# A routed feed-forward kernel on one core: x tile ahead of side columns, the first product's passes reordered, ScalarE's and VectorE's first pair reordered, a quarter of the mixing moved ahead of the first product

## The chip, the cores and the metric

The kernel runs on one core of one Trainium2 chip. The metric is the device time of one execution in microseconds. Before the change the median of three runs is 959.52 us (959.34 to 960.11).

## What is computed

The reference, cut to what matters (`x` is 128 x 64 x 1024 in float32; there are 8 conditioning kernels, 8 experts of rank 16, and 2 experts are chosen for each row):

```python
h = gelu(cond @ W0 + b0); h = gelu(h @ W1 + b1)
att = softmax(h @ W2 + b2)
agg_w = einsum('bk,koi->boi', att, weight)
y = einsum('boi,bih->boh', agg_w, x) + (att @ bias_k)[:, :, None]

base = einsum('bsd,od->bso', y, base_W)
probs = softmax(einsum('bsd,ed->bse', y, router_W))
w_dense = weights of the top 2 of probs, divided by their sum
mid = einsum('bsd,edr->bser', y, lora_A) * w_dense[..., None]
out = x + base + 2 * einsum('bser,erd->bsd', mid, lora_B)
```

## The kernel before

The rows (128 x 64) are taken in 64 tiles of 128 rows, two tiles to a "pair", 32 pairs. For each pair TensorE first mixes: `y = agg_w x`, with a 128 x 128 matrix `mix_w` for each tile. This is done in four quarters of four 128-column chunks (`mix_chunk(n, q, j)`, L483 to L497; quarter q reads `x_sb[q % 2]` and writes `y_ps[q % 2]`), and VectorE's `add_bias(n, q)` (L1122) moves a quarter from PSUM to `ya`, adding `bias_sb`. Then comes the large product of y with `base_W`. Each float32 operand is split into a high part (rounded, written by ScalarE, `*_hi`) and a low part (the rest, a subtraction on VectorE, `*_lo`), and each product is three passes: high by high, high by low, low by high. The blocks of the operand y are named A11, A12, A21, A22 and those of the weights B11, B21, B12, B22. From pair 2 on a seven-product scheme with sums of blocks (S1 to S4, T1 to T4) is used; pairs 0 and 1 use plain products (`plain_pair`, L623). The side columns (`side`, the columns of `lora_A` and of the router) are multiplied along: a product with them is a "head" of 376 columns (`plain_head`, L543) and a "tail" of 272 columns (`plain_tail`, L549), which holds the rest of the block and the side columns, and so needs the side columns' parts `side_hi_set` and `side_lo_set`. VectorE then chooses the experts from the logits (`route_logits`, `route_choice`, `route_weigh`, with `exponents` on ScalarE), makes `mid`, and `lora_B` (`lb_hi`, `lb_lo`) is multiplied with `mid`'s high and low parts.

There is no scheduler. The program of each engine is written out in its order, and engines wait for each other on semaphores; an engine that waits lets nothing behind it pass. What the change touches is the start, pair 0:

- SP (L266 to L278) issues the first loads on one queue: parameters, a block of weights (`a_raw`, B11), `x_sb[0]`, the side columns, `x_sb[1]`, three more blocks, `lora_B`, and a block for T1. `next_x(1)` (L280) loads pair 1's x tiles when quarters 2 and 3 of pair 0 have been mixed; `next_bias(1)` (L286) loads `bias_sb` for pair 1, after `bias_out`.
- GpSimd (POOL) makes the high and low parts of B11 (L366, L369), one half each at a time. Later it issues transfers that add a negated block to another in place (`add_to`, L372).
- TensorE mixes quarters 0 and 1, issues two warming matmuls (`keep_warm(2)`, L501), and enters `first_product` (L564), then a small bias product (L638), quarters 2 and 3, and the product of A21.
- ScalarE's `first_pair` (L964) and VectorE's `first_pair` (L1273) are lists of splits, negations and copies. The parts of a block of weights are written over the raw block in places, so a low part of B22 (`take_lo(B22, n)`) must wait until ScalarE has negated it (`neg_b22_set`). `keep_biases` (L920) copies the bias rows and issues their transfer to memory, at whose end `bias_out` rises.

Of the kernel before, what the change touches and what calls it, by code (L numbers as in the profile page):

```python
# [5 lines left out]
def adaln_ffn_kernel(nc, x, params, mix_t, bias_k, base_t, side, lora_b, out):  # L6
# [30 lines left out]
    HALF = 4  # L37
    WP = 2
# [19 lines left out]
    with ctx:  # L58
# [207 lines left out]
        def _(sp):  # L266
# [2 lines left out]
            sp.dma_start(bk_sb[:, :], bias_k).then_inc(bk_in, 16)  # L269
            sp.dma_start(a_raw, base_t[0, :, :]).then_inc(a_in, 16)  # L270
            sp.dma_start(x_sb[0][:, :], x_t[0, :, :]).then_inc(x_in[0], 16)
            sp.dma_start(w_raw[W_SIDE], side).then_inc(side_in, 16)
            sp.dma_start(x_sb[1][:, :], x_t[1, :, :]).then_inc(x_in[1], 16)
            sp.dma_start(b_raw, base_t[2, :, :]).then_inc(b_in, 16)
            sp.dma_start(c_raw, base_t[1, :, :]).then_inc(c_in, 16)
            sp.dma_start(d_raw, base_t[3, :, :]).then_inc(d_in, 16)
# [164 lines left out]
        def _(pe):  # L441
            def keep_warm(times):

                for _ in range(times):
                    nc.tensor.matmul(pb[:, 0:BANK], hot[:, 0:P], hot[:, :], start=True, stop=True)
# [52 lines left out]
            for q in range(2):  # L498
                for j in range(HALF):
                    mix_chunk(0, q, j)  # L500
            keep_warm(2)  # L501
            SPLITS = ((op_hi, w_hi), (op_hi, w_lo), (op_lo, w_hi))

            def wait_operand(o, p):
# [38 lines left out]
            def plain_head(y, w, start, stop, blk, to, j):  # L543

                at = blk * BLOCK + j * BANK
                nc.tensor.matmul(to[:, LEAD:BANK], y, w[:, at:at + HEAD], start=start, stop=stop,  # L546
                                 skip_group_check=True)
# [16 lines left out]
            def first_product():  # L564

                hi, lo = op_hi[A11], op_lo[A11]
                passes = [list(plain_splits(hi, lo, j, True)) for j in range(HALF)]
                pe.wait_ge(a11_first_set, 1)
                pe.wait_ge(op_hi_set[A11], 1)
                pe.wait_ge(w_hi_set[B11], WP)  # L570
                pe.wait_ge(side_hi_set, 1)
                for j in range(HALF):
                    plain_head(*passes[j][0], B11, pa, j)
                    plain_tail(*passes[j][0], B11, pa, j, 0)
                pe.wait_ge(op_lo_set[A11], 1)
                for j in range(HALF):
                    plain_head(*passes[j][2], B11, pa, j)
                    plain_tail(*passes[j][2], B11, pa, j, 0)
                for j in range(HALF):
                    if j % (HALF // WP) == 0:  # L580
                        pe.wait_ge(w_lo_set[B11], j // (HALF // WP) + 1)
                    plain_head(*passes[j][1], B11, pa, j)
                pe.wait_ge(side_lo_set, 1)
                for j in range(HALF):
                    plain_tail(*passes[j][1], B11, pa, j, 0)
# [37 lines left out]
            def plain_pair(p):  # L623
# [10 lines left out]
                if first(p):  # L634
                    first_product()
                    pe.wait_ge(bk_in, 16)
                    pe.wait_ge(bias_set, 2)
                    nc.tensor.matmul(bias_ps, att_t[:, :], bk_sb[:, :], start=True, stop=True).then_inc(bias_mm, 1)  # L638
                    for q in range(2, 4):
                        for j in range(HALF):  # L640
                            mix_chunk(0, q, j)
                else:
                    wait_operand(A11, p)
                    pe.wait_ge(plain_out, 1)
                    for j in range(HALF):
                        plain_with_side(*a11, B11, pa, j, 0, True)
# [208 lines left out]
        def _(act):  # L855
# [50 lines left out]
                               bias_bc[:, m * P:(m + 1) * P].rearrange("p (b s c) -> p b s c", s=2, b=PAR)  # L906
                               ).then_inc(bias_set, 1)
            place_mix(0, 1)
            act.wait_ge(side_in, 16)
            nc.scalar.activation(w_hi[W_SIDE], w_raw[W_SIDE], ACT.Copy).then_inc(side_hi_set, 1)  # L910

            def first_a11_high(m, done):

# [50 lines left out]
            def first_pair():  # L964
                first_a11_high(0, a11_first_set)
                first_a11_high(1, op_hi_set[A11])
                split_a21(0)
                act.wait_ge(att_rows_mm, 1)
                nc.scalar.copy(att_rows[:, :], pb[:, BANK:]).then_inc(att_rows_set, 1)
                act.wait_ge(b_in, 16)  # L970
                for n in range(WP):
                    take_hi(B21, n)
                keep_biases()
                split_high(A12, 0, y_ready, 4)
                split_high(A22, 0, y_ready, 4)
                act.wait_ge(a_in, 16)
                negate(T2, 0, neg_b11_set)
                act.wait_ge(c_in, 16)
                for n in range(WP):
                    nc.scalar.activation(w_hi[w_piece(T4, n)], w_raw[w_piece(T3, n)], ACT.Copy  # L980
                                         ).then_inc(b12_hi_set, 1)
                act.wait_ge(d_in, 16)
                for n in range(WP):
                    take_hi(B22, n)
                for m in range(2):
                    place_mix(1, m)
                negate(B22, 1, neg_b22_set)
                exponents(0)
                act.wait_ge(lb_in, 16)
                nc.scalar.activation(lb_hi[:, :], lb_raw[:, :], ACT.Copy).then_inc(lb_hi_set, 1)  # L990
                exponents(1)
# [68 lines left out]
        def _(dve):  # L1060
# [212 lines left out]
            def first_pair():  # L1273
# [20 lines left out]
                route_logits(0, pa[:, SLOG])  # L1294
                route_choice(0)
                route_weigh(0, pa[:, SMID])
                dve.wait_ge(neg_b22_set, WP)
                for n in range(WP):
                    take_lo(B22, n)
                add_bias(1, 0)  # L1300
                dve.wait_ge(lb_hi_set, 1)
                nc.vector.tensor_tensor(lb_lo[:, :], lb_raw[:, :], lb_hi[:, :].bitcast(f32),
                                        ALU.subtract).then_inc(lb_lo_set, 1)
# [157 lines left out]
```

## Time and profile before

| | us |
|---|---|
| median of the three runs | 959.52 |
| the profiled execution | 959.47 |
| its span, first to last instruction | 957.6 |
| TensorE (PE) busy | 949.1 (99%) |
| VectorE (DVE) busy | 741.8 (77%) |
| GpSimd (POOL) busy | 295.8 (31%) |
| ScalarE (ACT) busy | 237.8 (25%) |

The profile was taken in one execution. Times in the trace are microseconds from the span's start. The granted TensorE clock is 1.00 in all of the first 40 us. PEld is TensorE's loading of weights, which overlaps the matmuls. In a timeline a row is one instruction or several alike in a sequence (x4): its start, its length, engine, line, operation, what is written and read, the shapes, and in brackets for how long the engine sat idle before it and what ended that. Matmuls are pipelined: a recorded length runs past the start of the next, so that the time of a matmul in a sequence is read from start to start. In the chain of work the lengths add up.

### The profile page before, as it was taken

What the parts mean: (1) busy time and instruction counts of PE and PEld (TensorE: products, weight loads), DVE (VectorE), ACT (ScalarE), POOL (GpSimd) and SP (SyncE); (2) the same over time, 40 slices, a digit from 0 to 9 for tenths busy, and PEclk for the clock granted to TensorE, in tenths of its full rate; (3) what the DMA queues carried; (4) which work ended last, traced back from release to release, by engine and by line L of the source; (5) the groups of instructions that cost most, each with busy time, mean ns of one, the idle gap of its engine ahead of it and who ended that gap; (6) DMA issues with size and microseconds to landing.
All of it is one profiled execution on the core that took longest, in us unless ns stands there. A gap on an engine that the chain in (4) does not pass through costs nothing.

```text
span 957.6 us, 17843 instructions
## 1 busy us (share of the span) xinstructions
PE 949.1 (99%) x5777; PEld 876.6 (92%) x5777; DVE 741.8 (77%) x1641; ACT 237.8 (25%) x546; POOL 295.8 (31%) x230
## 2 busy tenths in 40 slices
PE   7999999999999999999999999999999999999998
PEld 6999999999999999999999999999999999999997
DVE  5778877877777877778777778777778777787775
ACT  5444222222212222222222122222222222222220
POOL 3012333123332133332233331333321333312331
PEclk9999999999999999999999999999999999999999
DMA  9766234423234332333332343333343323433311
GB/s 349 202 191 176 80 108 140 133 96 106 99 115 137 110 115 93 104 126 134 110 110 78 115 137 122 102 104 105 115 136 110 114 82 104 137 133 99 110 44 66
DMA packets 47125, 116.04 MB, mean 121 GB/s; under 512 B 20480, under 2 KB 20864, under 8 KB 45952
## 3 DMA queue, kind: packets, MB, share of 16 engines
q1 hardware_dynamic: 46112, 111.41, 35.0%
q0 software_dynamic: 576, 4.19, 2.3%
q8 instruction: 12, 0.20, 0.1%
q10 hardware_dynamic: 416, 0.16, 0.1%
q14 instruction: 9, 0.07, 0.0%
HBM read 77.97 MB, written 33.59 MB: 116 GB/s over the span
## 4 chain that ended last, share of the span: by engine, by line
PE 98%; DMA 1%; SPq 0%; issue 0%; ACT 0%; DVE 0%
PE pc L518 17%; PE pa L529 13%; PE pb L529 13%; PE y_ps L493 12%; PE pb L532 9%; PE pa L532 9%; PE pd L518 9%; PE pd L609 5%; PE pc L609 4%; PE pc L591 1%; PE pd L591 1%; DMA x_sb<-in_x 1%; PE pa L546 1%; PE pb L546 1%; PE pd L599 1%; PE pa L554 1%
## 5 line engine op out<-in xcount | busy, mean ns | idle before, releaser
L493 PE MATMUL y_ps<-mix_w,x_sb 128*128 128x128 f32 x1024 | 193.5, 273 | 1.0 <-DMA x_sb<-in_x 0.9
L409 POOL TENSOR_TENSOR out_sb<-out_sb,u 128x512 f32<-128x512 f32 x90 | 127.8, 1450 | 202.0 <-DVE u L1239 202.0
L493 PEld LDWEIGHTS y_ps<-mix_w,x_sb 128*128 128x128 f32 x1024 | 166.9, 188 | 13.3 <-DMA x_sb<-in_x 1.1
L379 POOL TENSOR_TENSOR ya<-ya 128x512 f32<-128x512 f32 x30 | 40.0, 1334 | 380.2 <-DVE ya L1142 380.2
L1142 DVE TENSOR_TENSOR ya<-y_ps,bias_sb 128x512 f32<-128x512 f32 x128 | 87.8, 686 | 38.3 <-PE y_ps L493 34.7
L518 PE MATMUL pc<-w_hi,s_hi 128*128 128x512 f32 x236 | 97.5, 413 | 0.0
L529 PE MATMUL pa<-w_hi,a_hi 128*128 128x376 f32 x240 | 94.6, 394 | 0.7 <-ACT p L956 0.7
L518 PE MATMUL pc<-w_hi,s_lo 128*128 128x512 f32 x236 | 92.8, 393 | 0.0
L518 PE MATMUL pc<-w_lo,s_hi 128*128 128x512 f32 x236 | 92.2, 391 | 0.0
L941 ACT ACTIVATE exps<-logits,neg_max 128x8 f32<-128x8 f32 x64 | 19.3, 301 | 260.6 <-DVE neg_max L1161 260.6
L948 ACT ACTIVATE mid_hi<-pd 128x128 fp32r<-128x128 f32 x61 | 16.9, 278 | 269.9 <-PE pd L599 269.9
L529 PE MATMUL pa<-w_hi,a_lo 128*128 128x376 f32 x240 | 80.2, 334 | 0.0
L529 PE MATMUL pa<-w_lo,a_hi 128*128 128x376 f32 x240 | 80.2, 334 | 0.0
L1153 DVE TENSOR_TENSOR a_lo<-ya,a_hi 128x512 fp32r<-128x512 f32 x96 | 67.9, 708 | 10.0 <-ACT a_hi L937 9.4
L532 PE MATMUL pa<-w_hi,a_hi 128*128 128x272 f32 x240 | 69.0, 288 | 0.0
L532 PE MATMUL pa<-w_lo,a_hi 128*128 128x272 f32 x240 | 69.0, 287 | 0.0
L532 PE MATMUL pa<-w_hi,a_lo 128*128 128x272 f32 x240 | 69.0, 287 | 0.0
L937 ACT ACTIVATE a_hi<-ya 128x512 fp32r<-128x512 f32 x95 | 59.5, 627 | 20.9 <-DVE ya L1142 20.9
L1204 DVE TENSOR_TENSOR out_sb<-pc,out_sb 128x512 f32<-128x512 f32 x92 | 62.5, 681 | 0.7 <-PE pc L609 0.7
L937 ACT ACTIVATE s_hi<-ya 128x512 fp32r<-128x512 f32 x60 | 37.7, 628 | 77.8 <-PE pb L532 77.1
L518 PE MATMUL pd<-w_hi,s_hi 128*128 128x512 f32 x120 | 56.8, 474 | 0.0
L1221 DVE TENSOR_TENSOR side_b<-pb,p 128x136 f32<-128x136 f32 x30 | 9.0, 300 | 60.7 <-PE pb L532 60.7
(236 smaller groups left out, 2561.1 us busy)
## 6 DMA issues: line engine op xcount, KB each, us to landing
x_sb<-in_x SPq DMA_DIRECT2D x64, 512.0 KB, 3.3
out_sb<-in_x SPq DMA_DIRECT2D x64, 512.0 KB, 4.4
out<-out_sb SPq DMA_DIRECT2D x62, 512.0 KB, 2.8
w_raw<-in_base_t SPq DMA_DIRECT2D x5, 1024.0 KB, 12.7
w_raw<-neg POOLq DMA_DIRECT2D x4, 1024.0 KB, 12.7
bias_sb<-bias_rows SPq DMA_DIRECT2D x62, 64.0 KB, 4.9
out<-out_sb SPq DMA_DIRECT2D x3, 256.0 KB, 2.0
w_raw<-in_side SPq DMA_DIRECT2D x1, 544.0 KB, 8.9
```

Source lines behind the costliest of these rows:

```text
L379: nc.gpsimd.tensor_tensor(y_block(0, 1), y_block(0, 1), y_block(0, 0), ALU.subtract).then_inc(s3_set, 1)
L409: nc.gpsimd.tensor_tensor(o, o, u2[:, :], ALU.add).then_inc(done, 1)
L493: mm = nc.tensor.matmul(y_ps[q % 2][:, j * P:(j + 1) * P], x_sb[m][:, c * P:(c + 1) * P], mix_w[m][:, :], start=True, stop=True)
L518: mm = nc.tensor.matmul(to[:, 0:BANK], y[o][:, j * P:(j + 1) * P], w[:, at:at + BANK], start=(begin and j == 0 and n == 0), stop=(j == HAL ...
L529: nc.tensor.matmul(to[:, LEAD:BANK], y[o][:, j * P:(j + 1) * P], w[:, at:at + HEAD], start=start, stop=stop, skip_group_check=True)
L532: mm = nc.tensor.matmul(to[:, BANK:BANK + 2 * SD].rearrange("p (a n) -> p a n", a=2), y[o][:, j * P:(j + 1) * P], tail, start=start, stop= ...
L609: mm = nc.tensor.matmul(to[:, :], m[:, :], w[:, cols], start=(begin and n == 0), stop=(n == 2), skip_group_check=True)
L937: nc.scalar.activation(op_hi[o][:, :], OPERAND[o], ACT.Copy).then_inc(op_hi_set[o], 1)
L941: nc.scalar.activation(exps[:, :], logits[:, :], ACT.Exp, bias=neg_max[:, :]).then_inc(exps_ready, 1)
L1142: nc.vector.tensor_tensor(to[:, :, :, m, :], y_ps[q % 2][:, :].rearrange("p (j s r) -> p j s r", j=HALF, s=2), bias_sb[m][:, :].rearrange( ...
L1153: nc.vector.tensor_tensor(op_lo[o][:, :], OPERAND[o], op_hi[o][:, :].bitcast(f32), ALU.subtract).then_inc(op_lo_set[o], 1)
L1204: nc.vector.tensor_tensor(o, src, o, ALU.add).then_inc(done, 1)
```

## The change

Five things are moved and nothing is added or removed. On SP `x_sb[1]` is loaded ahead of the side columns. On TensorE quarter 2 of pair 0's mixing stands ahead of the first product, and the first product runs its heads by themselves (high by high; half of high by low; low by high; the other half of high by low), and then the twelve tails. On ScalarE the high part of the side columns stands behind the two high parts of A11, the negation of B11 ahead of the bias rows and of A12, `place_mix(1, m)` ahead of B22, and `exponents(0)` ahead of the negation of B22. On VectorE `add_bias(1, 0)` stands ahead of the low parts of B22, whose wait is for each half by itself.

```diff
@@ SP
+            sp.dma_start(x_sb[1][:, :], x_t[1, :, :]).then_inc(x_in[1], 16)
             sp.dma_start(w_raw[W_SIDE], side).then_inc(side_in, 16)
-            sp.dma_start(x_sb[1][:, :], x_t[1, :, :]).then_inc(x_in[1], 16)
@@ TensorE
             keep_warm(2)
+            for j in range(HALF):
+                mix_chunk(0, 2, j)
@@ TensorE, first_product
                 pe.wait_ge(a11_first_set, 1)
                 pe.wait_ge(op_hi_set[A11], 1)
                 pe.wait_ge(w_hi_set[B11], WP)
+                def low_weights(n):
+                    pe.wait_ge(w_lo_set[B11], n + 1)
+                    for j in range(n * HALF // WP, (n + 1) * HALF // WP):
+                        plain_head(*passes[j][1], B11, pa, j)
+
+                for j in range(HALF):
+                    plain_head(*passes[j][0], B11, pa, j)
+                low_weights(0)
+                pe.wait_ge(op_lo_set[A11], 1)
+                for j in range(HALF):
+                    plain_head(*passes[j][2], B11, pa, j)
+                low_weights(1)
                 pe.wait_ge(side_hi_set, 1)
-                for j in range(HALF):
-                    plain_head(*passes[j][0], B11, pa, j)
-                    plain_tail(*passes[j][0], B11, pa, j, 0)
-                pe.wait_ge(op_lo_set[A11], 1)
-                for j in range(HALF):
-                    plain_head(*passes[j][2], B11, pa, j)
-                    plain_tail(*passes[j][2], B11, pa, j, 0)
-                for j in range(HALF):
-                    if j % (HALF // WP) == 0:
-                        pe.wait_ge(w_lo_set[B11], j // (HALF // WP) + 1)
-                    plain_head(*passes[j][1], B11, pa, j)
+                for n in (0, 2):
+                    for j in range(HALF):
+                        plain_tail(*passes[j][n], B11, pa, j, 0)
                 pe.wait_ge(side_lo_set, 1)
                 for j in range(HALF):
                     plain_tail(*passes[j][1], B11, pa, j, 0)
@@ TensorE, plain_pair
-                    for q in range(2, 4):
-                        for j in range(HALF):
-                            mix_chunk(0, q, j)
+                    for j in range(HALF):
+                        mix_chunk(0, 3, j)
@@ ScalarE
             place_mix(0, 1)
-            act.wait_ge(side_in, 16)
-            nc.scalar.activation(w_hi[W_SIDE], w_raw[W_SIDE], ACT.Copy).then_inc(side_hi_set, 1)
...
                 first_a11_high(1, op_hi_set[A11])
+                act.wait_ge(side_in, 16)
+                nc.scalar.activation(w_hi[W_SIDE], w_raw[W_SIDE], ACT.Copy).then_inc(side_hi_set, 1)
                 split_a21(0)
...
                     take_hi(B21, n)
+                act.wait_ge(a_in, 16)
+                negate(T2, 0, neg_b11_set)
                 keep_biases()
                 split_high(A12, 0, y_ready, 4)
                 split_high(A22, 0, y_ready, 4)
-                act.wait_ge(a_in, 16)
-                negate(T2, 0, neg_b11_set)
...
+                for m in range(2):
+                    place_mix(1, m)
                 act.wait_ge(d_in, 16)
                 for n in range(WP):
                     take_hi(B22, n)
-                for m in range(2):
-                    place_mix(1, m)
+                exponents(0)
                 negate(B22, 1, neg_b22_set)
-                exponents(0)
@@ VectorE
                 route_weigh(0, pa[:, SMID])
-                dve.wait_ge(neg_b22_set, WP)
+                add_bias(1, 0)
                 for n in range(WP):
+                    dve.wait_ge(neg_b22_set, n + 1)
                     take_lo(B22, n)
-                add_bias(1, 0)
```

How the instructions stand at the two places with most to do. TensorE, from the end of the mixing's quarter 1 (`x_sb_54` is `x_sb[1]`, `x_sb_53` is `x_sb[0]`; `pa` is the first product's bank) to the first product's wait for the low part of A11; before:

```order
17 L493 MATMUL y_ps<-mix_w_79,x_sb_54 128x128 [waits mix_set1,x_in1]
18 L493 MATMUL y_ps<-mix_w_79,x_sb_54 128x128 x3
19 L445 MATMUL pb<-hot 128x512 x2
20 L546 MATMUL pa<-w_hi,a_hi 128x376 [waits w_hi_set0,side_hi_set,op_hi_set0,a11_first_set]
21 L554 MATMUL pa<-w_hi,a_hi 128x272
22 L546 MATMUL pa<-w_hi,a_hi 128x376
23 L554 MATMUL pa<-w_hi,a_hi 128x272
24 L546 MATMUL pa<-w_hi,a_hi 128x376
25 L554 MATMUL pa<-w_hi,a_hi 128x272
26 L546 MATMUL pa<-w_hi,a_hi 128x376
27 L554 MATMUL pa<-w_hi,a_hi 128x272
28 L546 MATMUL pa<-w_hi,a_lo 128x376 [waits op_lo_set0]
```

and now:

```order
19 L445 MATMUL pb<-hot 128x512 x2
20 L493 MATMUL y_ps<-mix_w_78,x_sb_53 128x128 [waits y_ready]
21 L493 MATMUL y_ps<-mix_w_78,x_sb_53 128x128 x3
22 L548 MATMUL pa<-w_hi,a_hi 128x376 [waits w_hi_set0,op_hi_set0,a11_first_set]
23 L548 MATMUL pa<-w_hi,a_hi 128x376 x3
24 L548 MATMUL pa<-w_lo,a_hi 128x376 [waits w_lo_set0]
25 L548 MATMUL pa<-w_lo,a_hi 128x376
26 L548 MATMUL pa<-w_hi,a_lo 128x376 [waits op_lo_set0]
27 L548 MATMUL pa<-w_hi,a_lo 128x376 x3
28 L548 MATMUL pa<-w_lo,a_hi 128x376 [waits w_lo_set0]
29 L548 MATMUL pa<-w_lo,a_hi 128x376
30 L556 MATMUL pa<-w_hi,a_hi 128x272 [waits side_hi_set]
```

Quarter 2's four chunks stand ahead of the product, the wait for the side columns has gone from the first matmul to the first tail, and six heads instead of four heads and four tails stand ahead of the wait for the low part of A11 (`op_lo_set0`).

ScalarE, from the copy of the side columns or the high parts of A11 to the high parts of B12, before:

```order
17 L910 ACTIVATE w_hi<-w_raw 128x1088 [waits side_in]
18 L916 ACTIVATE a_hi<-ya 128x4x64 [waits y_ready] x2
19 L962 ACTIVATE a_hi<-ya 128x512 [waits y_ready]
20 L969 COPY att_rows<-pb 128x512 [waits att_rows_mm]
21 L861 ACTIVATE w_hi<-w_raw 128x1024 [waits b_in]
22 L861 ACTIVATE w_hi<-w_raw 128x1024
23 L923 COPY bias_rows_sb<-pd 128x64 [waits bias_mm]
24 L925 DMA bias_rows<-bias_rows_sb 128x2x32 [waits bias_ready]
25 L937 ACTIVATE a_hi<-ya 128x512 [waits y_ready] x2
26 L867 ACTIVATE neg_106<-w_raw 128x1024 [waits a_in]
27 L867 ACTIVATE neg_106<-w_raw 128x1024
28 L980 ACTIVATE w_hi<-w_raw 128x1024 [waits c_in]
```

and now:

```order
17 L919 ACTIVATE a_hi<-ya 128x4x64 [waits y_ready] x2
18 L971 ACTIVATE w_hi<-w_raw 128x1088 [waits side_in]
19 L965 ACTIVATE a_hi<-ya 128x512 [waits y_ready]
20 L974 COPY att_rows<-pb 128x512 [waits att_rows_mm]
21 L866 ACTIVATE w_hi<-w_raw 128x1024 [waits b_in]
22 L866 ACTIVATE w_hi<-w_raw 128x1024
23 L872 ACTIVATE neg_106<-w_raw 128x1024 [waits a_in]
24 L872 ACTIVATE neg_106<-w_raw 128x1024
25 L926 COPY bias_rows_sb<-pd 128x64 [waits bias_mm]
26 L928 DMA bias_rows<-bias_rows_sb 128x2x32 [waits bias_ready]
27 L940 ACTIVATE a_hi<-ya 128x512 [waits y_ready] x2
28 L985 ACTIVATE w_hi<-w_raw 128x1024 [waits c_in]
```

The copy of the side columns has gone behind the high parts of A11, and the two negations (`neg_106`) ahead of the bias rows' copy and transfer.

## Rows read from the trace of the kernel before

**Rows 1.** The chain of work that ended last: shares of the span by engine.
```profile
PE 98%; DMA 1%; SPq 0%; issue 0%; ACT 0%; DVE 0%
```
**Rows 2.** Waits of TensorE over the span: us in total, times, longest.
```profile
PE pa L529 <- ACT p L956: 0.7, 1, 0.7
```
**Rows 3.** Timeline of TensorE, 13 to 22 us.
```profile
13.27 1.16 PE L493 MATMUL y_ps<-mix_w,x_sb 128*128 128x128 f32 x8 [0.90 <-DMA x_sb<-in_x]
14.19 0.71 PE L445 MATMUL pb<-hot 128*128 128x512 f32 x2
15.78 0.41 PE L546 MATMUL pa<-w_hi,a_hi 128*128 128x376 f32 x1 [0.88 <-issue]
...
19.53 0.43 PE L638 MATMUL pd<-bk_sb,att_t 8*128 8x64 f32 x2
19.89 2.05 PE L493 MATMUL y_ps<-mix_w,x_sb 128*128 128x128 f32 x16
21.70 0.42 PE L546 MATMUL pb<-w_hi,a_hi 128*128 128x376 f32 x1
```
**Rows 4.** The chain in order of time: start, us, what.
```profile
18.41 0.69 PE pa L546 x4
...
29.95 0.09 issue
30.05 0.46 PE y_ps L493 x2
...
31.39 0.22 PE y_ps L493 x2
```
**Rows 5.** Timeline of ScalarE.
```profile
11.99 0.51 ACT L880 COPY mix_w<-summed 64x64 f32<-64x64 f32 x2
12.52 1.11 ACT L910 ACTIVATE w_hi<-w_raw 128x1088 fp32r<-128x1088 f32 x1
...
20.24 0.44 ACTq L925 DMA_DIRECT2D bias_rows<-bias_rows_sb  x1
...
29.45 1.03 ACT L880 COPY mix_w<-summed 64x64 f32<-64x64 f32 x4
```
**Rows 6.** Timeline of SP, whose rows are the issues of transfers.
```profile
3.01 0.44 SPq L272 DMA_DIRECT2D w_raw<-in_side  x1
...
24.66 0.90 SPq L290 DMA_DIRECT2D bias_sb<-bias_rows  x2
```
**Rows 7.** From issue to landing, us: side columns; pair 1's `bias_sb` (its tile's view).
```profile
w_raw<-in_side SPq DMA_DIRECT2D x1, 544.0 KB, 8.9
...
DMA to landing us min/median/max: 5.8/7.9/10.0
```
**Rows 8.** Timeline of VectorE.
```profile
14.54 0.69 DVE L1142 TENSOR_TENSOR ya<-y_ps,bias_sb 128x512 f32<-128x512 f32 x1 [1.37 <-PE y_ps L493]
15.78 0.98 DVE L1153 TENSOR_TENSOR a_lo<-ya,a_hi 128x512 fp32r<-128x512 f32 x1 [0.55 <-ACT a_hi L916]
...
33.89 2.35 DVE L1064 TENSOR_TENSOR w_lo<-w_raw,w_hi 128x1024 fp32r<-128x1024 f32 x2
...
40.40 0.28 DVE L1199 TENSOR_TENSOR mid_lo<-pd,mid_hi 128x128 fp32r<-128x128 f32 x1
...
80.83 4.36 DVE L1064 TENSOR_TENSOR w_lo<-w_raw,w_hi 128x1024 fp32r<-128x1024 f32 x2
```
**Rows 9.** Timeline of GpSimd.
```profile
11.53 4.69 POOL L369 TENSOR_TENSOR w_lo<-w_raw,w_hi 128x1024 fp32r<-128x1024 f32 x2
...
80.25 1.63 POOL L397 TENSOR_TENSOR s<-s,ya 128x512 f32<-128x512 f32 x1
81.84 2.27 POOL L400 TENSOR_TENSOR ya<-ya,s 128x512 f32<-128x512 f32 x1
```
**Rows 10.** Timeline of TensorE, 33 to 42 us.
```profile
33.45 0.38 PE L493 MATMUL y_ps<-mix_w,x_sb 128*128 128x128 f32 x2
...
41.03 0.42 PE L617 MATMUL pa<-lb_hi,mid_hi 128*128 128x376 f32 x1
```

More of the change, by code:

```diff
@@ L570, in first_product @@
                 pe.wait_ge(w_hi_set[B11], WP)
-                pe.wait_ge(side_hi_set, 1)
+                def low_weights(n):
+                    pe.wait_ge(w_lo_set[B11], n + 1)
+                    for j in range(n * HALF // WP, (n + 1) * HALF // WP):
+                        plain_head(*passes[j][1], B11, pa, j)
                 for j in range(HALF):
                     plain_head(*passes[j][0], B11, pa, j)
-                    plain_tail(*passes[j][0], B11, pa, j, 0)
+                low_weights(0)
                 pe.wait_ge(op_lo_set[A11], 1)
@@ L577, in first_product @@
                     plain_head(*passes[j][2], B11, pa, j)
-                    plain_tail(*passes[j][2], B11, pa, j, 0)
-                for j in range(HALF):
-                    if j % (HALF // WP) == 0:
-                        pe.wait_ge(w_lo_set[B11], j // (HALF // WP) + 1)
-                    plain_head(*passes[j][1], B11, pa, j)
+                low_weights(1)
+                pe.wait_ge(side_hi_set, 1)
+                for n in (0, 2):
+                    for j in range(HALF):
+                        plain_tail(*passes[j][n], B11, pa, j, 0)
                 pe.wait_ge(side_lo_set, 1)
```

## The prediction

> **What bounds the kernel now.** Read the chain of work first: 98% of it is TensorE [rows 1], so a part of the change counts only where it removes or makes an idle stretch of TensorE. The view of waits comes next: the last one of TensorE in the whole span that it lists is 0.7 us for ScalarE's copy of `pa` [rows 2]; that copy follows TensorE's own product, in the third pair, and moves with it. All others lie before the first product. What the change can win is therefore at the start, which the timelines show.
>
> TensorE mixes quarter 1 of pair 0 at 13.27, after 0.90 us of waiting for the transfer of `x_sb`; two warming matmuls follow at 14.19; the first product starts at 15.78, after 0.88 us of waiting [rows 3]. At 19.53 stands the bias product, at 19.89 quarters 2 and 3 of the mixing, 1.81 us together, and at 21.70 the second product [rows 3]. Nothing waits between 15.78 and 21.70. One small wait more: the first mixing matmuls of pair 1 start at 30.05 when ScalarE's two copies into `mix_w` (half of 1.03 us from 29.45, so 29.95) are done. In the chain they take 0.46 us instead of 0.22, after a gap of 0.09: 0.33 us of waiting in all [rows 4, 5].
>
> **x ahead of the side columns.** The side columns, issued at 3.01, landed 8.9 us later, at 11.9 [rows 6, 7]; the second x tile, next on the queue, just before the 13.27 of the matmul that waited for it [rows 3]. One tile is 512 KB and the side columns are 544 KB, so changing places lets x land at about 11.9 and the side columns at 13.2. Then another thing is last: the second `mix_w` is written by ScalarE at 11.99 + 0.51 = 12.50 [rows 5]. With the 0.1 us from the end of such a copy to its matmul, 29.96 to 30.05 [rows 4, 5], quarter 1 starts at 12.6, 0.67 us sooner. VectorE's bias add, ScalarE's second high part of A11 and the head that waits for it follow each other directly, so the add goes from 14.54 to 13.87 and the first product from 15.78 to 15.11 [rows 3, 8]. ScalarE's copy of the side columns (1.11 us [rows 5]) now stands behind that high part, 15.0 to 16.1, on data that landed at 13.2.
>
> **The third quarter of mixing ahead of the first product.** Its condition, one finished bias add, is met at 13.2. It starts behind the two warming matmuls (recorded 0.71 us from 14.19, so from 13.52 then) at 14.0 to 14.2 and takes half of 1.81 us, to 15.1 at the latest, inside what was a wait. This takes 0.90 us from after the first product. It also sets free `x_sb` for the load of pair 1 some 6 us sooner, but that load stands behind the weights on the same queue of SP, and so should land as before.
>
> **The first product's order.** The work is the same, 12 matmuls of 376 columns ("heads") and 12 of 272 ("tails"), 15.78 to 19.53 = 3.75 us without a wait; a head takes 0.17 us (four in 0.69 [rows 4]), and for the first after a wait I allow 0.08 more. Now four heads with high parts and two with the low weights (GpSimd's first half, ready after half of 4.69 us from 11.53, at 13.9 [rows 9]) run from 15.11 to 16.2 (6 x 0.17 + 0.08 = 1.10). Then the low part of A11 is wanted. Here is the choice on which the number hangs. VectorE's subtraction for it ran from 15.78 to 16.76, 0.98 us, where the add of the same size at 14.54 took 0.69; GpSimd's two subtractions ran to 11.53 + 4.69 = 16.22 [rows 8, 9]. 16.76 is 0.54 us behind that end, within one undisturbed instruction. The same is seen at 80.83: two VectorE subtractions take 4.36 us, where two like them took 2.35 at 33.89, beside two of GpSimd [rows 8, 9]. Let each engine wait for the other's whole instruction: VectorE waits to 81.88, works 1.07 us; GpSimd waits for that and ends at 84.11; VectorE's second ends 1.08 us later, at 85.19, the recorded end. So I take it that VectorE does not get through before GpSimd ends: however early it is asked, the low part is ready at 16.76. The Trainium skill (SBUF — State Buffer, section "SBUF: two separate sides") has such a rule: a VectorE instruction with two SBUF inputs and a GpSimd one that reads SBUF share a pair of ports under an exclusive lock, and the later of the two is blocked until the other ends. By that rule, the trace agreeing at both places, the head start that the change gives this subtraction is spent on waiting, and the sum stays 1.25 us; were the engines only slowed, it would be 1.9 us, rival 1.
>
> TensorE then waits from 16.2 to 16.86, and has 3.75 - 1.10 = 2.65 us left, to 19.51: only 0.02 us sooner than now. The side columns' low parts (VectorE, directly behind, of 1088 columns, so little over half of the 2.35 us of 33.89, to 18.0) are wanted at 19.0; no wait. Bias product 0.36 us, quarter 3 0.90 us: the second product starts at 20.78 against 21.70, **0.92 us sooner**.
>
> **ScalarE's first pair reordered.** ScalarE starts on A21's high part later now, by the side copy, and, its instructions laid end to end from 16.1, ends the high parts of B21 at about 19.1 and the negation of B11 at 21.0. VectorE follows as now, since its low part of A11 is not sooner. By my estimate from the rows of like size A12 is ready at about 23.5 and wanted some 3.6 us (twelve pairs of head and tail) after 20.8: covered. `place_mix` for pair 1 now runs before B22, done for its first tile at about 26.0 and wanted at 28.8: **the 0.33 us at 30.05 goes**. The negation of B22 goes behind `exponents(0)`, ending near 31.8. All this is cover at no price: if B22's low part were late it would show as a wait of `pc<-w_lo` at 36.
>
> **VectorE's bias add first.** `add_bias(1, 0)` now stands before B22's low parts. It waits for TensorE's mixing quarter, whose last matmuls end at 33.83 now [rows 10] and at 32.6 then, and for `bias_sb`. Queued behind it are B22's low parts, `lb_lo`, the second routing and `mid_lo`; these and the add took from 33.89 to 40.68, 6.8 us, without a wait [rows 8]: `mid_lo` at 39.5. TensorE wants it at 41.03 - 1.25 = 39.8 [rows 10]: covered, by 0.2 to 0.3 us.
>
> **Sum.** 0.92 + 0.33 = 1.25 us. The profiled execution took 959.47 us (span 957.60 and 1.87 around it), 0.05 below the median of the three runs, 959.52. It gives 958.22 and 958.27: I say 958.3. About 0.2%, 1.9 us, is what a measurement can tell from no change, so this is "the same".
>
> **Rivals.** (1) VectorE is not held up: it works slower beside GpSimd but ends 0.98 us after it starts. The low part is then ready at 15.11 + 0.98 = 16.09, TensorE never waits, and the gain is 1.25 + 0.65 = 1.9 us: 957.6. For it: the durations overlap in the record. Against it: both places give ends that fit exclusion to 0.05 us. Chance 0.15, half of it past the bound.
>
> (2) The other side: `bias_sb` is late and holds VectorE's queue. ScalarE issued the copy of the bias rows to memory at 20.24 [rows 5], and SP the load that waits for it at 24.66 [rows 6]; now the copy stands behind the negation, at about 21.25, and the load at 25.7. Its first half landed 5.8 us after its issue and the second 10.0 [rows 7]. With 5.8 it lands at 31.5, with 10.0 at 35.7; VectorE wants it at 32.6. Past 32.8 each microsecond is one of TensorE's, past 34.1 the gain is gone; at 35.7 TensorE's wait is 2.9 us and the time 959.52 - 1.25 + 2.9 = 961.2, and past 36.0 it is slower by over 0.2%. For it: GpSimd's accumulating transfer of T1 is no longer held by the negation of B11 and starts up to 2 us sooner, closer to this load. Against it: the load stands behind pair 1's two x tiles, as now, and those come no later. Chance 0.10, half of it slower than before, a quarter past the bound.
>
> (3) Only the mixing quarter is won and something small comes back (B21's or A12's parts, `mid_lo` by its 0.2 us of cover): 0.25 to 1.2 us less gain, 958.6 to 959.5. Chance 0.20. That the order does nothing at all is excluded, as the quarter does move into a wait of 0.9 us.
>
> The forecast itself has 0.55. The transfers' landings can shift by a few tenths.
>
> **How the numbers follow.** The range reaches down to rival 1 with 0.1 us for noise, 957.5, and up through rival 3 with 0.2 us for the spread of runs, 959.7; outside are most of rival 2 and little else. Faster by over 0.2% (under 957.6): half of rival 1 and little of the rest, 0.10. Slower by over 0.2% (over 961.4): 0.04. Else 0.86.
>
> **What would show it.** In the timeline after: quarter 1 at 12.6; quarter 2 of the mixing at 14.0; first head at 15.1; VectorE's first `a_lo` lasting about 1.6 us and ending at 16.76; a wait of TensorE of 0.65 us before the first `w_hi,a_lo`; second product at 20.8; no wait at the first mixing matmuls of pair 1 (28.8); every later TensorE row 1.25 us sooner. An `a_lo` that ends near 16.1 would prove rival 1; an add of pair 1 that begins after 32.8, ended by a transfer, rival 2. A time under 957.5 or over 959.7 would prove the sum wrong.

## The result and the profile after

| | before | after |
|---|---|---|
| median, us | 959.52 (22 runs, 959.31 to 960.12) | 961.44 (22 runs, 958.33 to 963.72) |
| the profiled execution, us | 959.47 | 961.68 |
| its span, us | 957.6 | 959.8 |

The ratio is 1.0019, with a 95% interval of 1.0013 to 1.0025: the change makes the kernel slower, by 1.9 us or 0.2%, which is about the least that can be told from no change. It also spreads the runs over 5.4 us where they lay within 0.8. The granted clock is 1.00 in both profiled executions.

The waits of TensorE over the span of the changed kernel (us in total, times, longest), but for 2.7 us and 0.2 us at the very start:

```profile
PE pc L597 <- DVE w_lo L1069: 1.7, 1, 1.7
PE pa L623 <- DVE mid_lo L1204: 1.1, 1, 1.1
PE pa L531 <- ACT p L959: 0.7, 1, 0.7
PE pa L548 <- DVE a_lo L1158: 0.4, 1, 0.4
PE y_ps L493 <- ACT mix_w L885: 0.3, 1, 0.3
```

The first two are what no part of the forecast had: VectorE is late with the low parts of B22 and with `mid_lo`. The last two are the wait for the low part of A11, which was forecast, and a short one that follows x's earlier landing. The chain of work, by engine:

```profile
PE 96%; DMA 2%; DVE 1%; ACT 1%; issue 0%; POOL 0%; DVEq 0%; POOLq 0%
```

It was 98% TensorE [rows 1]. The 2% of transfers are two. The same chain in order of time (start, us, what):

```profile
19.00 1.89 ACT neg L872 x2
20.89 0.11 ACT bias_rows_sb L926
21.02 6.84 DMA bias_rows<-bias_rows_sb
27.87 8.34 DMA bias_sb<-bias_rows
...
36.29 0.06 DVE ya L1147
...
36.90 2.35 DVE w_lo L1069 x2
39.25 1.13 DVE lb_lo L1307
...
42.82 0.29 DVE mid_lo L1204
43.11 0.14 issue
43.24 0.41 PE pa L623
```

This is one path from end to end: ScalarE's negation, the copy of the bias rows to memory (6.8 us), the load of `bias_sb` that waits for it (8.3 us), VectorE's first bias add of pair 1, and all that is queued behind that add. TensorE's timeline, with the rows that answer to [rows 3, 4, 10]:

```profile
12.71 1.13 PE L493 MATMUL y_ps<-mix_w,x_sb 128*128 128x128 f32 x8 [0.27 <-ACT mix_w L885]
...
14.14 1.05 PE L493 MATMUL y_ps<-mix_w,x_sb 128*128 128x128 f32 x8
15.19 0.93 PE L548 MATMUL pa<-w_hi,a_hi 128*128 128x376 f32 x4
15.96 0.51 PE L548 MATMUL pa<-w_lo,a_hi 128*128 128x376 f32 x2
16.84 0.97 PE L548 MATMUL pa<-w_hi,a_lo 128*128 128x376 f32 x4 [0.37 <-DVE a_lo L1158]
...
20.87 0.42 PE L548 MATMUL pb<-w_hi,a_hi 128*128 128x376 f32 x1
...
28.97 0.38 PE L493 MATMUL y_ps<-mix_w,x_sb 128*128 128x128 f32 x2
...
38.16 0.50 PE L597 MATMUL pc<-w_hi,a_hi 128*128 128x512 f32 x1 [1.70 <-DVE w_lo L1069]
...
43.24 0.41 PE L623 MATMUL pa<-lb_hi,mid_hi 128*128 128x376 f32 x1 [1.14 <-DVE mid_lo L1204]
```

Up to 28.97 all goes as forecast to within 0.2 us: the mixing of pair 1 starts 1.08 us sooner than in [rows 4]. Then the product with `lora_B` starts at 43.24 against 41.03 [rows 10], 2.21 us later, and 2.2 us is what the span grew by. VectorE, for [rows 8]:

```profile
15.20 1.59 DVE L1158 TENSOR_TENSOR a_lo<-ya,a_hi 128x512 fp32r<-128x512 f32 x1 [0.55 <-ACT a_hi L919]
...
36.29 0.69 DVE L1147 TENSOR_TENSOR ya<-y_ps,bias_sb 128x512 f32<-128x512 f32 x1 [4.68 <-DMA bias_sb<-bias_rows]
36.90 2.35 DVE L1069 TENSOR_TENSOR w_lo<-w_raw,w_hi 128x1024 fp32r<-128x1024 f32 x2
```

Finally the three issues that matter, on ScalarE's queue, SP's and GpSimd's (for [rows 5, 6]; GpSimd's stood at 26.37 before):

```profile
21.02 0.47 ACTq L928 DMA_DIRECT2D bias_rows<-bias_rows_sb  x1
27.87 1.71 SPq L290 DMA_DIRECT2D bias_sb<-bias_rows  x2
25.39 1.01 POOL L374 DMA_DIRECT2D w_raw<-neg  x1 [9.16 <-DMA w_raw<-in_base_t]
```

The load of `bias_sb` is issued 3.2 us later than before, and GpSimd's accumulating transfer of T1 (1 MB) 1.0 us sooner. The load used to be issued 1.7 us ahead of T1's transfer; now it comes 2.5 us behind it. How the DMA queues fared between 27 and 31 us (queue and kind: packets, MB, share of the 16 engines' time; q0 is GpSimd's, q1 is SP's), before:

```profile
q1 hardware_dynamic: 409, 0.37, 37.3%
```

and after:

```profile
q0 software_dynamic: 109, 0.89, 113.0%
q10 hardware_dynamic: 10, 0.00, 0.2%
q1 hardware_dynamic: 1, 0.00, 0.0%
```

### The profile page after: what moved, and what is told of

The parts are those of the page before. It is cut to its first block, busy times and chain, and to the rows that moved or that the text cites. A ratio compares the mean times of both kernels' runs of the same rounds, so it can differ in the third digit from the quotient of the medians.

```text
span 959.8 us, 17843 instructions
## 1 busy us (share of the span) xinstructions
PE 949.8 (99%) x5777; PEld 876.9 (91%) x5777; DVE 742.3 (77%) x1641; ACT 238.0 (25%) x546; POOL 295.7 (31%) x230
## 4 chain that ended last, share of the span: by engine, by line
PE 96%; DMA 2%; DVE 1%; ACT 1%; issue 0%; POOL 0%; DVEq 0%; POOLq 0%
PE pc L520 17%; PE pa L531 13%; PE pb L531 13%; PE y_ps L493 11%; PE pb L534 9%; PE pa L534 9%; PE pd L520 9%; PE pd L615 5%; PE pc L615 4%; PE pd L597 1%; DMA bias_sb<-bias_rows 1%; DMA bias_rows<-bias_rows_sb 1%; PE pd L605 1%; PE pc L597 1%; PE pb L445 0%; PE pb L548 0%
```

## The experiments

The first theory (A): the load of `bias_sb` loses to T1's transfer, and VectorE's add, now at the head of its queue, hands the delay on. Its rival (B): the bias rows leave later, behind the negation, and that alone makes the load late. A second rival (C): pair 1's early x load, which the moved mixing quarter lets SP issue at 15.2 in place of 21.1, crowds the queue. In the recorded expectations A1 stands for A, and D (once B') for C; "Theory C" in the first of them is another one, that ScalarE's order is at fault. No experiment leaves out or changes any part of the computation.

### One part of the change undone, or one transfer held

**VectorE's bias add back behind B22's low parts.**

```diff
-                add_bias(1, 0)
                 for n in range(WP):
                     dve.wait_ge(neg_b22_set, n + 1)
                     take_lo(B22, n)
+                add_bias(1, 0)
```

> The changed kernel with one line put back on VectorE: add_bias(1, 0) behind B22's low parts. Theory A (the transfer of pair 1's bias_sb lands at about 36.2 instead of 30.5, and VectorE, waiting for it at the head of its queue, holds back B22's low parts, lb_lo and mid_lo): B22's low parts run from about 31.6 to 34, TensorE's wait of 1.7 us before pc with w_lo goes; the add still starts near 36.3, so lb_lo, the second routing and mid_lo still follow it (4.5 us, to 40.9) and TensorE, which now wants mid_lo at 39.8, waits about 1.1 us more: 959.5, between 959 and 960. Theory C (the bias transfer is innocent, something in ScalarE's order makes B22's parts late): the time stays near 961.4.

Measured: 958.71 us (958.27 to 960.15), ratio 0.9994 (0.9985 to 1.0003). 2.7 us of the changed kernel's time are back, more than was expected of A (959 to 960), and the spread has shrunk. In the profiled execution, 958.27, the fastest of its runs, `bias_sb` landed at 33.3, against 36.2 in the changed kernel, and the add ran at 33.79 without a wait. So in most runs the loss needs the add at the head of the queue. Why some still go up to 960.15 was not seen; that a load can be late enough for an add in its old place is shown below, by the quarter alone.

**T1's transfer held until `bias_sb` has landed** (the changed kernel, one wait more on GpSimd).

```diff
                 pool.wait_ge(neg_b11_set, WP)
+                pool.wait_ge(bias_in[0], 16)
                 add_to(T1, 0, t1_made)
```

> The changed kernel, but GpSimd starts the accumulating transfer of T1 only when bias_sb of pair 1 has landed. Theory A1 (that transfer, moving from 26.6 to 32, takes the DMA engines while bias_sb waits): bias_sb, issued at 27.9, lands 3.4 to 5.8 us later, at 31.3 to 33.7, VectorE's wait of 4.7 us shrinks to under 2, and the time is 958.2 to 959.4. Theory B (bias_sb is late because its copy to memory is issued 0.8 us later and takes 6.8 instead of 4.4 us): only a part of the lateness hangs on T1, the landing stays near 36 and the time near 961.4.

Measured: 958.47 (958.28 to 960.4), ratio 0.9992 (0.9983 to 1.0001). In the profiled execution the load was issued at 27.60, hardly sooner than the 27.87 of the changed kernel, but landed in 5.9 us in place of 8.3. This speaks for A: the issue was as late, and the time was back.

**The bias rows back ahead of the negation**, the direct test of B.

```diff
+                keep_biases()
                 act.wait_ge(a_in, 16)
                 negate(T2, 0, neg_b11_set)
-                keep_biases()
```

> The changed kernel, but keep_biases is back ahead of the negation of B11 on ScalarE. The bias rows' copy to memory is issued at about 20.0 instead of 21.0. Theory B: it lands by 24.6, bias_sb is issued by 24.7 and lands by 30.5 to 31.5 as before the change; the whole loss goes, 958.2 to 958.6. Theory A1 (T1's transfer is the cause): it still begins near 26.6 and meets bias_sb, which stands behind pair 1's x tiles to 27.6; the landing is at 32 to 36 and the time 959 to 961.4.

Measured: 961.31 (960.18 to 963.53), ratio 1.002 (1.0011 to 1.003). Nothing is won: B alone falls. SP's, GpSimd's and VectorE's timelines of this kernel:

```profile
25.11 1.73 SPq L290 DMA_DIRECT2D bias_sb<-bias_rows  x2
...
23.41 1.01 POOL L374 DMA_DIRECT2D w_raw<-neg  x1 [7.17 <-ACT neg L872]
...
34.77 0.69 DVE L1147 TENSOR_TENSOR ya<-y_ps,bias_sb 128x512 f32<-128x512 f32 x1 [2.57 <-DMA bias_sb<-bias_rows]
```

The load is issued at 25.11, 2.8 us sooner than in the changed kernel, but T1's transfer is still ahead of it, at 23.41, and the load takes 9.6 us.

**Pair 1's first x load held until all of pair 0 is mixed**, the test of C.

```diff
-                    sp.wait_ge(mixed, 4 * n + m - 1)
+                    sp.wait_ge(mixed, 4 if first_load else 4 * n + m - 1)
```

> The changed kernel, but the load of x_sb[0] for pair 1 is held until all four quarters of pair 0 are mixed (about 20.9), as late as before the change. Theory D (that load, issued at 15.2 instead of 21.1, keeps SP's queue full when the bias rows go to memory, so that their copy takes 6.8 us instead of 4.4): the copy takes 4.4 to 5, bias_sb is issued at about 25.7 and the time falls to 958.3 to 960. Theories A1 and B: nothing changes by more than 0.5 us, near 961.4.

Measured: 959.97 (958.37 to 962.9), ratio 1.001 (1.0001 to 1.002): between the two, and spread over 4.5 us. In the profiled execution (961.3) T1's transfer was issued at 24.90 and the load at 28.92, after a copy of the bias rows that took 7.9 us. So the copy was no shorter for it in that execution. Holding the x load wins 1.5 us in the median, but most runs stay slower than before: it is not what decides here.

**Both cures together** (the add behind, T1's transfer held).

> The changed kernel with both cures: add_bias(1, 0) behind B22's low parts on VectorE, and GpSimd's transfer of T1 held until bias_sb of pair 1 has landed. Theory A (VectorE's wait for bias_sb, made long by T1's transfer, is the whole loss): no run is far above the fastest, the median is 958.3 (958.2 to 958.5), against 958.7 and 958.5 for the cures alone. If another cause remains, the median stays above 958.6 with runs of 959 to 960 among them.

Measured: **958.33 (958.19 to 958.54)**, ratio 0.9988 (0.9979 to 0.9997). That is the time that was forecast for the change, and the spread is gone with the loss. TensorE's product with `lora_B` starts at 39.87 there, against 41.03 before (1.16 us sooner) and 43.24 after: the changed kernel lost 3.37 us between 36 and 43 us.

### One part alone, in the kernel before

**The negation of B11 ahead of the bias rows.**

> The kernel before with one part of the change: the negation of B11 ahead of keep_biases on ScalarE. Theory A1 (the negation ahead lets T1's transfer start when T1 has landed, at 23 to 25.4 instead of 26.4, and the bias rows go out 2 us later): bias_sb lands at 33 to 36 or later instead of 30.5. In the kernel before VectorE asks for it only at 36.2, so that most of it is hidden: 959.5 to 960.0, with single runs up to 961. Theory B' (the lateness comes from the early x load or the order of SP's loads): bias_sb lands at 30.5 to 32.

Measured: 959.18 (959.04 to 960.16), ratio 0.9998 (0.999 to 1.0007). T1's transfer was issued at 24.36, ahead of the load at 25.64, and the load took 10.0 us, to 35.6. The add, still behind B22's low parts, ran at 35.74, and TensorE has no wait between 29 and 46 us: the late load is there and costs nothing. The time is even below the 959.5 to 960.0 expected, since with the negation gone from there ScalarE writes `mix_w` for pair 1 at 27.45 in place of 29.45, and TensorE's wait at that mixing is gone.

**VectorE's bias add ahead of B22's low parts.**

> The kernel before with one part of the change: add_bias(1, 0) ahead of B22's low parts on VectorE. Theory A: the place of the add is harmless as long as bias_sb lands in time, and here it lands at 30.5: the add waits for the mixing's quarter to 33.9, mid_lo is ready at 40.7 to 40.8, TensorE wants it at 41.0: 959.5 (959.3 to 959.8). Rival: the add at the head of the queue costs by itself, 0.2 us or more of waiting before the product with lora_B: 959.8 and over.

Measured: 959.44 (959.26 to 960.12 but for one far-off run), ratio 1.000 (0.9991 to 1.0009). The load was issued at 24.40, ahead of T1's transfer at 26.25, landed at 30.2, and the add ran at 33.77. The add's new place is there and costs nothing.

**Quarter 2 of the mixing ahead of the first product.**

> The kernel before with one part of the change: quarter 2 of pair 0's mixing ahead of the first product. By the prediction's sum it takes 0.90 us from behind the first product and fits into the wait ahead of it (14.7 to 15.6): 958.6 (958.4 to 958.9). If a part of it pushes the first product, the gain is 0.6 or less: 958.9 and over.

Measured: 961.03 (958.86 to 962.37 but for one far-off run); the ratio, 1.0008 (0.9999 to 1.0017), doesn't tell it from no change. This expectation was a miss: neither the negation nor the add has been moved here, and yet most runs are slower. Four of twelve lie at 958.86 to 958.94, as expected, the others from 960.3 up. The profiled execution is one of those, 962.37; SP's and VectorE's rows:

```profile
26.92 1.38 SPq L290 DMA_DIRECT2D bias_sb<-bias_rows  x2
...
38.73 0.69 DVE L1143 TENSOR_TENSOR ya<-y_ps,bias_sb 128x512 f32<-128x512 f32 x1 [3.12 <-issue]
```

The copy of the bias rows took 6.8 us in place of 4.4, so the load was issued at 26.92, behind T1's transfer (25.75), and landed after 11.7 us, at 38.6: too late even for an add in its old place. The same kernel was then run with each of the two transfers held.

**The quarter ahead, T1's transfer held.**

> The kernel before with quarter 2 of the mixing ahead of the first product (as b5, which came out at 961.0 with runs from 958.9 to 962.4), and GpSimd's transfer of T1 held until bias_sb of pair 1 has landed. Theory A1 (there too T1's transfer starves the load of bias_sb, which is issued after 26.9): bias_sb lands by 34, VectorE's add starts when its queue reaches it, no run stands far above the fastest, median 958.8 (958.7 to 959.1), the 0.6 to 0.9 us of the quarter. If T1's transfer is not the cause there: still 960 to 962.

Measured: 958.94 (958.86 to 959.37), ratio 0.9996 (0.9987 to 1.0005). The load was issued at 26.53 and took 5.9 us.

**The quarter ahead, pair 1's x load held.**

> The kernel before with quarter 2 of the mixing ahead of the first product (as b5), and the load of x_sb[0] for pair 1 held until quarter 3 is mixed, with T1's transfer as it was. Theory D (the early x load makes the bias rows' copy to memory land 6.8 us after its issue instead of 4.4, so that bias_sb is issued behind T1's transfer instead of ahead of it): the copy lands near 24.6, bias_sb is issued ahead of T1's transfer and the time is 958.8 (958.7 to 959.2). If the x load is innocent: 960 to 962 as b5.

Measured: 958.88 (958.78 to 958.97), ratio 0.9994 (0.9985 to 1.0003). The copy of the bias rows took 3.8 us, the load was issued at 23.95, ahead of T1's transfer, and took 5.6. So here C is what tips the order, and either cure is enough.

This pair shows the race most plainly, since T1's transfer was issued at the same time in both (25.75 and 25.76). The DMA queues from 27 to 31 us, the quarter alone:

```profile
q0 software_dynamic: 96, 0.79, 99.2%
```

and with the x load held:

```profile
q1 hardware_dynamic: 340, 0.36, 28.0%
```

Whichever was issued first has this stretch for itself, even where, as in the second, the engines are 28% busy. From 31 us on, in the second kernel, both move.

### The order put right without holding T1's transfer

The changed kernel with the bias rows ahead of the negation and the x load held, the add left ahead.

> The changed kernel with both things put back that delay the bias rows' copy: keep_biases ahead of the negation, and the x load held; T1's transfer is free to start when T1 has landed (23 to 25.4). Theory of a race (what counts is which of the two, the load of bias_sb or T1's transfer, is in the queues first, and the negation behind keep_biases lets T1's transfer go only after 22.8): the median falls below a3's 961.3 and a4's 960.0, to 958.4 to 959.5, with some runs above 960 left. Theory A1 in its strict form (T1's transfer alone decides): 960 to 961.5.

Measured: 959.16 (958.35 to 963.05), ratio 1.0002 (0.9992 to 1.0012). It doesn't settle: five of eleven runs lie at 958.35 to 958.87, the rest from 959.16 up. In the profiled one (958.35) SP was first by 0.13 us:

```profile
24.83 0.90 SPq L290 DMA_DIRECT2D bias_sb<-bias_rows  x2
...
24.96 1.01 POOL L374 DMA_DIRECT2D w_raw<-neg  x1 [8.71 <-DMA w_raw<-in_base_t]
...
32.72 0.69 DVE L1147 TENSOR_TENSOR ya<-y_ps,bias_sb 128x512 f32<-128x512 f32 x1 [0.51 <-PE y_ps L493]
```

The load landed in 4.6 us, and the add waited for TensorE alone. With a lead of 0.13 us the order can turn from run to run; that the slower runs are those in which it turned was not seen, since only one run is profiled.

### What all profiles say of the race

Each row is one profiled execution (the last experiment, below, went as "both cures"): when the two transfers were issued, and from issue to landing, in us. `bias_sb` is loaded in two halves; the first is meant, for which the add waits.

| kernel | `bias_sb` issued | T1's issued | `bias_sb` took | T1's took |
|---|---|---|---|---|
| before | 24.66 | 26.37 | 5.8 | 16.1 |
| add alone | 24.40 | 26.25 | 5.8 | 15.9 |
| quarter, x held | 23.95 | 25.76 | 5.6 | 16.5 |
| rows first, x held | 24.83 | 24.96 | 4.6 | 10.9 |
| T1's held | 27.60 | 34.11 | 5.9 | 9.3 |
| both cures | 26.77 | 33.10 | 5.7 | 9.4 |
| quarter, T1's held | 26.53 | 33.04 | 5.9 | 9.2 |
| add behind | 25.81 | 23.10 | 7.5 | 8.0 |
| rows first | 25.11 | 23.41 | 9.6 | 7.9 |
| negation alone | 25.64 | 24.36 | 10.0 | 9.0 |
| x held | 28.92 | 24.90 | 6.9 | 8.7 |
| **after** | 27.87 | 25.39 | 8.3 | 7.9 |
| quarter alone | 26.92 | 25.75 | 11.7 | 9.6 |

Where the load was issued first it took 4.6 to 5.9 us; where T1's transfer was, 6.9 to 11.7. In those six the load landed 2.2 to 3.4 us after T1's transfer did (after: 25.39 + 7.9 = 33.3, then 36.2). So the load's landing isn't a price of its own, as [rows 7] had seemed to give it: it depends on which of two queues was first. T1's issue moves too: with the negation ahead it waits for the load of T1's block in most profiles, and came at 23.10 to 25.39 without any edit to that load.

### VectorE beside GpSimd

The last experiment takes the reading that the sum rested on and uses it. Both cures, and GpSimd's second half of B11's low part cut in two pieces, the last of which waits until VectorE has made the low part of A11; the first product's second low weights move behind eight tails (this part of the edit isn't shown).

```diff
+            for n in (2, 3):
+                if n == 3:
+                    pool.wait_ge(op_lo_set[A11], 1)
...
+                mm = nc.gpsimd.tensor_tensor(w_lo[:, to], w_raw[:, of], w_hi[:, to].bitcast(f32), ALU.subtract)
```

> The version with both cures (958.33), and GpSimd's second half of B11's low part cut in two, its last piece held until VectorE has made the low part of A11, with the first product's second low weights behind the tails. If VectorE's subtraction is shut out while GpSimd's runs (the prediction's reading): it now starts at 15.2 and takes 0.69 us instead of 1.5 to 1.6, TensorE's wait of 0.3 to 0.6 us before the first a_lo goes, and the time is 958.0 (957.8 to 958.3). If it is only slowed by sharing, it takes about 1 us or its old 1.5; if GpSimd's late piece in turn holds VectorE's side columns, TensorE waits 0.2 to 0.5 us ahead of the last tails and nothing is won: 958.3.

Measured: **957.84 (957.75 to 957.89)**, ratio 0.9983 (0.9974 to 0.9992): 1.6 us under the kernel before, 3.6 under the changed one, and the fastest of all. Timelines of VectorE and GpSimd:

```profile
15.13 0.69 DVE L1167 TENSOR_TENSOR a_lo<-ya,a_hi 128x512 fp32r<-128x512 f32 x1 [0.55 <-ACT a_hi L928]
...
13.86 1.29 POOL L376 TENSOR_TENSOR w_lo<-w_raw,w_hi 128x512 fp32r<-128x512 f32 x1
15.90 1.29 POOL L376 TENSOR_TENSOR w_lo<-w_raw,w_hi 128x512 fp32r<-128x512 f32 x1 [0.75 <-DVE a_lo L1167]
```

With GpSimd idle the subtraction takes 0.69 us, not 1.59, TensorE no longer waits for it, and its second product starts at 20.36 against 20.87 after and 20.86 with both cures. The overlap has moved to VectorE's next subtraction, that of the side columns:

```profile
16.06 2.28 DVE L1133 TENSOR_TENSOR w_lo<-w_raw,w_hi 128x1088 fp32r<-128x1088 f32 x1 [0.24 <-ACT w_hi L980]
```

It takes 2.28 us beside GpSimd's last piece where it took 1.28 before, and nothing of TensorE's waits for it.

## Why the prediction was wrong

The forecast was 958.3, within 0.2% of before. What came is 961.44, and with it rival 2, which had a chance of 0.10: "`bias_sb` is late and holds VectorE's queue".

**The start: right.** Quarter 1 at 12.71 (12.6 forecast), quarter 2 at 14.14 (14.0), the first head at 15.19 (15.1), the second product at 20.87 (20.8), and no wait at the mixing of pair 1. Of the differences 0.07 us is a later start of the first mixing, at 11.35 against 11.28 before. The low part of A11 took 1.59 us (1.6 forecast) and ended at 16.79. The wait for it is recorded as 0.37 us; from start to start the first head behind it, at 16.84, is 0.54 us later than six heads without a wait would have put it (16.3).

**The gain: nearly right, though two parts of the change won nothing.** Both cures together give 958.33, a gain of 1.1 us where 1.25 was forecast. The quarter alone is worth 0.9 at the second product: it starts at 20.69 to 20.71 in the three kernels with the quarter alone, against 21.59 in both kernels without it (negation alone, add alone) and 21.70 before. In the three with it the first product started at 15.12, 15.58 and 15.70, as x landed sooner or later, and it made no difference: its wait for the low part of A11 took it back. With x ahead and the first product's passes reordered as well it starts at 20.86 (both cures): 0.15 us later. The sum had said of x ahead that it wins nothing ("the head start that the change gives this subtraction is spent on waiting"). The reordering loses by the rows: ahead of the same wait it puts six heads (1.1 us) where four heads and four tails (15.78 to 17.05, nearly 1.3 us) stood. The rest of the gain is ScalarE's: with the negation alone TensorE's wait at pair 1's mixing is gone already, while with the quarter alone TensorE arrives sooner at pair 1's mixing and waits 0.47 us there, so that the quarter by itself wins only 0.5 us (958.88 and 958.94).

**The step that failed** is in VectorE's part: the landing of `bias_sb`, which the sum put at no cost. It called it covered, on the ground given against rival 2, "the load stands behind pair 1's two x tiles, as now, and those come no later". The x tiles did not delay it. Issued at 25.7 and 5.8 us long, as forecast, it would have been there at 31.5; it landed at 36.2, and TensorE waited 1.7 us for B22's low parts and 1.1 us for `mid_lo`. Three things did it, each of which stood in the text by itself:

- The copy of the bias rows, issued at 21.02 (21.25 forecast), took 6.8 us, not 4.4. Only its issue had been moved in the text, and its length kept. The x load, which "should land as before", is in SP's queue from 15.2 on; with the quarter alone, holding it brings the copy from 6.8 back to 3.8 us. In the kernel with all of the change but the x load held it took 7.9, so this can't be all of it.
- T1's transfer came 1.0 us sooner. Rival 2 had this ("starts up to 2 us sooner, closer to this load") but not that the two change places. By its own figures they could: T1's transfer at 24.4 at the earliest, the load at 25.7. The load went from 1.7 us ahead to 2.5 us behind, and behind it moves only when T1's transfer is nearly done.
- The add was put at the head of VectorE's queue, with B22's low parts and `mid_lo` behind it. In the kernel before, 10.0 us for the load cost nothing (negation alone); with the add ahead, a load that took 9.6 (rows first) costs 1.9 us against both cures (960.18 and 958.31, both profiled).

The price that rival 2 gave was right. It put the point at which cover ends at a landing at 32.8; the load landed at 36.2, 3.4 us past it, and the changed kernel lost 3.37 us against the one with both cures. The other three kernels with the add ahead and a late load fit as well: landings 0.7, 1.9 and 3.0 us past 32.8 (T1's held, rows first, x held) put the product with `lora_B` at 40.52, 41.72 and 42.84, which is 0.65, 1.85 and 2.97 us behind both cures' 39.87. That its 961.2 lies near 961.44 is in part luck: the load was issued 2.2 us later than it had it and took 1.7 us less than its 10.0. What was wrong was the chance. The two landings, 5.8 and 10.0, stood in [rows 7]; the question of what made the second of them 4.2 us longer, in the kernel before, was not asked. T1's first packets moved at 31 to 32 us in that trace, while the second load was still in flight.

**The range** ended at 959.7, since it left most of rival 2 out. The only rows on this load gave 5.8 and 10.0 us, and with 10.0 the text's own price was 961.2; that belonged inside the range.

**Exclusion of VectorE and GpSimd: right.** In twelve profiled kernels GpSimd works until 16.2; the subtraction begins anywhere from 15.12 to 15.78 and lasts 1.67 to 0.98 us, but ends at 16.76 to 16.80 in each. In a thirteenth (T1's held) GpSimd ended 0.2 us later, and so did the subtraction, at 16.96. With GpSimd held it takes 0.69. By the Trainium skill (SBUF — State Buffer, section "SBUF: two separate sides"), the later of the two engines is blocked for the whole of the other's instruction; the runs here agree but for 0.1 us, since the subtraction ends 0.55 us after GpSimd's where it takes 0.69 us by itself.

## What to carry to other kernels

Two transfers that are issued within a few microseconds of each other have an order as well as a length, and an edit that moves either issue can turn it: list the issues of all queues around the place, before and after, and price the landing for both orders. An instruction that waits for a transfer belongs behind work that doesn't, unless its landing has a margin larger than its spread. And where the runs of a change spread where those of before did not (5.4 us against 0.8 here), look for a race between queues first.

## What the runs showed of the hardware

**The transfer that was issued second stood still for some microseconds.** Between 27 and 31 us q0 had 109 packets and q1 one in the changed kernel; before, q1 had 409 and q0 none, although T1's transfer had been issued at 26.37. It does not stand still until all ahead of it is done: from 31 us on, before, T1's transfer moved beside the second half of `bias_sb` (landed at 35.1) and the loads behind it. From 32 to 36 us:

```profile
q0 software_dynamic: 54, 0.44, 53.1%
q1 hardware_dynamic: 236, 0.55, 35.1%
```

By the Trainium skill (DMA: Bandwidth & Descriptors, section "Queues, rings and completion order") each DMA engine goes round its queues packet by packet, which would let both move. The windows from 31 us on fit that, and those from 27 to 31 us don't, but for the kernel where the two were issued within 0.13 us: from 27 to 32 us q0 had 83 packets there and q1 471. Whether the second one's packets wait at the engines or reach them late, no run here tells. With T1's transfer first the engines were full (99 to 113%); with the load first they were 28 to 37% busy while T1's stood still, which speaks against waiting at the engines. It stays open.

**An accumulating transfer's length depends on its turn.** T1's 1 MB took 7.9 to 9.6 us where it was issued ahead of `bias_sb` or after its first half had landed, and 15.9 to 16.5 where `bias_sb` was ahead by 1.7 us or more.

**Small copies vary.** The bias rows' 32 KB, from ScalarE's issue to SP's issue that waits for it, took 3.8 to 7.9 us over the 14 profiles: 4.8 to 6.9 with pair 1's early x load, and both 3.8 (quarter, x held) and 7.9 (x held) without it. What sets it is open.
